# Local attention of six layers on one core: scores ahead of the last tile's weight turn, the next queries normalised ahead of the softmax's sums

## The reference

```python
q, k, v = split(shift_tokens(x) @ Wqkv[i])          # 16 heads of 64 channels
q = l2norm(q) * q_scale[i];  k = l2norm(k) * k_scale[i]
q = q * cos * scale + rotate_half(q) * sin * scale
k = k * cos / scale + rotate_half(k) * sin / scale
out = local_attention(q, k, v)   # windows of 32: each sees itself and the one before, softmax
x = out @ Wo[i] + x
x = feed_forward(shift_tokens(x)) + x               # layer norm, 341 hidden, gelu gate
```

## Time and profile before

| | |
|---|---|
| median of 3 runs | 3145.54 us (3144.41 to 3152.8) |
| the profiled execution | 3135.21 us, its span 3133.4 us |
| granted TensorE clock, mean | 0.971 |
| TensorE busy | 2802.7 us, 89% of the span |
| VectorE busy | 2594.8 us, 83% |
| ScalarE busy | 2238.7 us, 71% |
| GpSimd busy | 1365.0 us, 44% |

### The profile page before, as it was taken

The page is one execution under the profiler, slowest core; times in us unless marked ns, Lnnn a source line. Parts: engine busy times, 40 slices in busy tenths (PEclk is TensorE's granted clock), DMA queues, the critical chain, the costliest instruction groups (busy, mean ns, idle before and its releaser), DMA issues. The chain is left out here.

```text
span 3133.4 us, 74866 instructions
## 1 busy us (share of the span) xinstructions
PE 2802.7 (89%) x29085; PEld 1564.2 (50%) x29181; DVE 2594.8 (83%) x3866; ACT 2238.7 (71%) x3690; POOL 1365.0 (44%) x818
## 2 busy tenths in 40 slices
PE   3999898998898989879998998999899899999998
PEld 1233333333333333346655665666476656655764
DVE  4999889888887788469968996998699779968995
ACT  2277777767656667768867886887688778867884
POOL 0200333523335210056645664666466546646661
PEclk8699999999999999989999999999999999999999
DMA  3200001010010020011111111111111111111110
GB/s 112 69 1 2 1 8 32 1 32 8 9 32 2 21 68 2 2 39 41 36 43 43 35 35 44 42 35 57 29 35 36 57 29 35 35 50 35 39 38 21
DMA packets 62995, 101.21 MB, mean 32 GB/s; under 512 B 20450, under 2 KB 45216, under 8 KB 61472
## 3 DMA queue, kind: packets, MB, share of 16 engines
q1 hardware_dynamic: 62636, 96.26, 11.0%
HBM read 38.30 MB, written 7.34 MB: 15 GB/s over the span
## 5 line engine op out<-in xcount | busy, mean ns | idle before, releaser
L914 DVE TENSOR_REDUCE a_part<-ps 128x1 f32<-128x512 f32 (+3 forms) x1664 | 984.9, 652 | 157.8 <-PE ps L594 150.9
L890 ACT ACTIVATE a_Pb<-ps 128x1024 f32<-128x1024 f32 (+3 forms) x832 | 762.7, 974 | 347.8 <-PE ps L760 346.4
L1265 PE MATMUL ps<-early 128*128 128x512 f32 x1152 | 555.7, 615 | 76.7 <-DVE l_qn L1656 60.1
L1202 POOL TENSOR_TENSOR l_sine<-l_qn,stack 128x512 f32<-128x512 f32 x192 | 344.1, 1792 | 201.2 <-DVE l_qn L1656 193.5
L1226 POOL TENSOR_TENSOR l_weights<-l_weights,l_rcp 128x1024 f32<-128x1024 f32 x96 | 182.7, 1903 | 476.1 <-DVE l_rcp L1694 476.1
L594 PE MATMUL ps<-stack,a_QS 48*128 48x512 bf16 x1024 | 312.7, 405 | 72.2 <-DMA a_QS<-pieces 30.0
L1265 PEld LDWEIGHTS ps<-early 128*128 128x128 f32 x1152 | 205.0, 191 | 301.9 <-issue 144.9
L1645 DVE TENSOR_REDUCE l_norm<-l_square 128x8 f32<-128x512 f32 x384 | 252.8, 683 | 114.4 <-ACT l_square L1486 107.1
L1486 ACT ACTIVATE l_square<-ps 128x512 f32<-128x512 f32 x384 | 226.1, 594 | 89.0 <-PE ps L1265 87.8
L1665 DVE TENSOR_TENSOR l_cosine<-l_qn,stack 128x1024 f32<-128x1024 f32 x192 | 282.3, 1470 | 4.1
L644 PE MATMUL ps<-a_Pb,V 128*32 128x256 f32 (+1 forms) x3968 | 279.7, 398 | 0.0
(11 more groups left out here) (214 smaller groups left out, 5065.7 us busy)
## 6 DMA issues: line engine op xcount, KB each, us to landing
l_V_earlier<-l_V SPq DMA_DIRECT2D x96, 384.0 KB, 3.5
l_V_earlier<-l_V SPq DMA_DIRECT2D x96, 128.0 KB, 3.3
early<-in_L_ffn_Wqkv_dram SPq DMA_DIRECT2D x6, 1536.0 KB, 8.3
a_QS<-pieces SPq DMA_DIRECT2D x96, 64.0 KB
pieces<-a_piece SPq DMA_DIRECT2D x6, 512.0 KB, 2.6
pieces<-early SPq DMA_DIRECT2D x12, 256.0 KB, 2.7
a_KS<-pieces SPq DMA_DIRECT2D x48, 64.0 KB
l_w_o<-in_L_ffn_Wo_dram SPq DMA_DIRECT2D x6, 512.0 KB, 4.0
```

The source lines that it names most:

```text
L890: e.activation(Pb[:, n % 2, 2 * p:2 * p + 2, lo:CH], ps[:, 2 * p:2 * p + 2, lo:CH], ACT.Exp)\
L914: e.tensor_reduce(part[:, u % 2, column(h, qt), b:b + 1], bank[:, 0:width], AX.X, ALU.max)\
L1202: e.tensor_tensor(sine[:, :, 0:ROT], swap[:, :, ROT:LD], table[:, :, 0:ROT], ALU.mult).then_inc(s.rotated, 1)
L1265: e.matmul(ps[:, (V_BANK[T] if i == 2 else 0) + b, :], XS[:, T * P:(T + 1) * P], w_qkv[:, at:at + CH], start=True, stop=True).then_inc(s.v ...
```

## The change

The order of the instructions of `attend` is changed on three engines; no instruction is added, removed or altered.

- TensorE: `scores(T)` go ahead of `turn_weights(T - 1)`, and the projection of the queries of `T + 2` goes ahead of `values(T - 1)`.
- ScalarE: `place_low(T - 1, 0)` goes behind the inverse norms of the keys of `T + 1`; `store_o(T - 1)` goes behind the exponentials and the inverse norms of the queries of `T + 2`.
- VectorE: `place_high(T - 1)` goes behind `subtract(T)`; `normalise` of the queries of `T + 2` goes ahead of `sums(T)`.

```diff
--- before.py
+++ after.py
@@ -1376,17 +1376,17 @@
                         if ahead:
                             project(l, T + 1, 1, 0)
                             project(l, T + 1, 1, 1)
+                        scores(l, T, 0)
+                        scores(l, T, 1)
                         if T:
                             turn_weights(l, T - 1, 0)
                             turn_weights(l, T - 1, 1)
-                        scores(l, T, 0)
-                        scores(l, T, 1)
+                        if T + 2 < NT:
+                            project(l, T + 2, 0, 0)
+                            project(l, T + 2, 0, 1)
                         if T:
                             values(l, T - 1, 0)
                             values(l, T - 1, 1)
-                        if T + 2 < NT:
-                            project(l, T + 2, 0, 0)
-                            project(l, T + 2, 0, 1)
                         if ahead:
                             project(l, T + 1, 2, 0)
                             project(l, T + 1, 2, 1)
@@ -1559,21 +1559,20 @@
                         if ahead:
                             squares(l, T + 1, 1, 0)
                             squares(l, T + 1, 1, 1)
-                        if T:
-                            place_low(l, T - 1, 0)
                         if ahead:
                             inverse_norms(l, T + 1, 1)
                         if T:
+                            place_low(l, T - 1, 0)
                             place_low(l, T - 1, 1)
-                        if T:
-                            store_o(l, T - 1, 0)
-                            store_o(l, T - 1, 1)
                         if T + 2 < NT:
                             squares(l, T + 2, 0, 0)
                             squares(l, T + 2, 0, 1)
                         exponentials(l, T)
                         if T + 2 < NT:
                             inverse_norms(l, T + 2, 0)
+                        if T:
+                            store_o(l, T - 1, 0)
+                            store_o(l, T - 1, 1)
                         if ahead:
                             store_values(l, T + 1)
                     place_low(l, NT - 1, 0)
@@ -1723,20 +1722,21 @@
                             residual(l, T - 2)
                         if ahead:
                             sum_squares(l, T + 1, 1)
-                        if T:
-                            place_high(l, T - 1, 0)
                         if ahead:
                             normalise(l, T + 1, 1)
                         maxima(l, T)
                         subtract(l, T)
+                        if T:
+                            place_high(l, T - 1, 0)
                         if T + 2 < NT:
                             sum_squares(l, T + 2, 0)
                         if ahead:
                             cosines(l, T + 1, 1)
                             add_rotated(l, T + 1)
+                        if T + 2 < NT:
+                            normalise(l, T + 2, 0)
                         sums(l, T)
                         if T + 2 < NT:
-                            normalise(l, T + 2, 0)
                             cosines(l, T + 2, 0)
                     residual(l, NT - 2)
                     centre(l, 0)
```

## The result

The changed kernel is slower: 3197.4 us median of 4 runs (3186.35 to 3205.33) against 3144.97 us, a ratio of 1.0159 (95% interval 1.013 to 1.0188). The forecast was 3179 us in a range of 3150 to 3207. In the changed kernel VectorE's lines from `sum_squares` to `place_high`, and `residual`, stand one line higher (the cosines are L1664, the reciprocal L1693).

A forecast was written before the change was run, and what follows sets the result against it. A ring of waits over GpSimd's sequence was to set the pace: tiles from 15.32 to 15.64 us gave 25 us, layer starts 7, ends 1. Sum +33 on 3145.5: 3179 us, range 3150 to 3207.

The forecast's parts named there:

- GpSimd's sequence behind the reciprocal: Product, two sines, addition, two sines of the next keys; ends 10.63 us after the reciprocal, with 1.83 us of slack.
- the meeting at the port: VectorE's cosines and GpSimd's sines of the keys exclude each other at the SBUF port; sines end 0.95 us later.
- the hold: The wait of keys' cosines and sines for each other, 0.95 us; rival without it: 3105 us, chance 0.09.
- the ring: Steady tile, reciprocal to reciprocal over GpSimd's sines, add_rotated, normalisation and sums: 15.64 us instead of 15.32; chance 0.73.
- a ring of 15.8: Upper end of the forecast case in which GpSimd's ring sets the pace, priced at 3192 us.
- the 0.22: Wait of add_rotated after the end of GpSimd's second sine, some 0.22 us, read from a layer's last tile.
- The order at the port: Queries' cosines ahead of GpSimd's product, keys' cosines between the two sines; the order was said hardly to matter.
- A hold for the whole instruction: Rival: each hand-over at the port costs the full instruction, giving 16.06 us a tile and 3211 us; chance 0.07.
- TensorE's ring: Rival: TensorE's steady-tile ring, maxima through values, projections and scores, sets the pace at 15.20 us; 3144 us, chance 0.11.
- What scores ahead are worth: With scores ahead of the turn of weights on TensorE, maxima could start about 1.04 us sooner in each tile.
- The end of a layer: Reciprocal of tile 13 to the last turn of weights: 27.7 us instead of 27.54, 1 us for six layers.
- The start of a layer: The reciprocal of tile 0 comes 1.20 us later in each layer, 7 us for six layers.

The follow-up runs named there:

- e5: The changed kernel, but from a layer's tile 1 on VectorE sums the keys by heads into a spare tile instead of multiplying by the cosine table: 3179.02 us.
- e1: The changed kernel with VectorE's normalisation of the next queries put back behind the softmax's sums: 3181.38 us.
- e3: The changed kernel with sums ahead of the next queries' normalisation, and VectorE's copy of the turned weights ahead of the maxima in every tile: 3097.68 us.
- e4: The kernel before with one move alone, VectorE's normalisation of the next queries ahead of the softmax's sums: 3301.83 us.
- e2: The changed kernel with VectorE's copy of the turned weights ahead of the maxima in a layer's last two tiles alone: 3177.93 us.
- e6: The kernel before with only the next queries' projection ahead of values on TensorE and store_o late on ScalarE: 3113.52 us.

## Why the prediction was right, point by point

**The bound.** Right. GpSimd's sequence behind the reciprocal had 1.83 us of slack, the meeting at the port and the normalisation used 0.95 + 1.20 of it, and the tile came out at 15.64 us, as worked out. e5 takes the hold out, and the ring shows bare at the start of a layer, at 14.66 us where 14.69 was due. e1 takes the normalisation out, and the wait for GpSimd goes; the bare ring of 14.44 on the path forecast is not seen there. Single links were off by about 0.1 us in both directions: the held product ended 2.83 us after the reciprocal (forecast 2.94), the last sine 11.46 (11.58), and the normalisation starts 0.03 us after the addition's end instead of overlapping it. That such errors cancel to the second decimal is luck. So is, in part, that the time lies in the range: the tiles gave 22.0 of the 25 us forecast, and the starts and ends of the layers 33.8 where 8 was forecast. (3192, the price of a ring of 15.8, should be 3191.)

Two readings rested on rows that don't carry them. The cosines at 1884.43 took their full 1.23 us, so they hardly waited behind a sine, and the idling ahead of 1887.00, from which I took the 0.22, is put down to TensorE's turn (L1281). The changed kernel bears both out: its held cosines ran ahead of the next sine, and 0.22 us lie between the end of the last sine (2030.16) and `add_rotated` (2030.38).

**The order at the port.** Right: cosines ahead of the product, then first sine, cosines, second sine. The page "SBUF — State Buffer" of the Trainium skill, section "Who interferes with whom", says that issue order decides who blocks, and the trace agrees: the cosines, queued at 2027.32, went ahead of the sine of 2027.91. A hold for the whole instruction would have made 16.06 us by the prediction's estimate, and the 1.09 us that the held cosines took after the sine's end say why it was 15.64. The same section of the Trainium skill says that a VectorE instruction with at most one input from SBUF, outside its 2-port modes, does not contend with GpSimd; e5 agrees, with 1.28 us for the sine beside such a reduction.

**TensorE's ring.** Mis-sized by 0.19 us (15.39 for 15.20), and its closing wait misplaced. It hid behind GpSimd's ring in the changed kernel, as forecast, and capped e1 and e5. Its cause is the copy behind the subtraction: e3 moves it ahead and the ring is gone.

**What scores ahead are worth.** I priced the move as a gain of TensorE's that the other ring hides. e4 shows that the normalisation without the other moves costs far more, since the product then stands ahead of the scores, the values and the queries' projection; I had not followed that ring. Whether the scores' move or the projection's opens it is not shown, so what scores ahead are worth stays open.

**The end of a layer.** The term that failed: 1 us for six layers, 19.3 measured. I had priced the new order of instructions at their durations of before, and missed that in the steps of tiles 14 and 15 `values` have no projection of queries ahead of them to hide the wait for the copy (2.52 and 2.49 us of idling above). The clock I had priced at nothing; behind that idling it fell to its lower level, in all six ends. e2 takes the idling away and gets 19.5 us back in the median (3197.4 to 3177.9). The 1 us either way that I allowed was too narrow.

**The start of a layer.** The reciprocal of tile 0 came 2.4 us later on average, where 1.2 was forecast for the normalisation; e1, which takes it out, gives 1.35 a layer back. The rest goes along with the granted clock, which fell at the start of each of the six layers and of two in the kernel before, and with TensorE's first turn in the second to fifth layer, which starts after 2.5 to 3.1 us of idling at the loop's jump instead of 1.05 to 1.4. The kernels with a changed order on TensorE show this idling (e2, e3 and e5, and e1 and e6 in three of four layers), e4 with the old order doesn't, though its clock fell at all six starts too. No experiment tells what makes the jump longer, or what each of the two costs; this is open.

## What to carry to other kernels

Before a step is put ahead of another on one engine, follow what waits for the later one once around the ring: here 1.2 us of VectorE's own time stood ahead of a reciprocal from which two thirds of a tile of GpSimd's work hang, and the row that decides is the slack of that sequence, not the idle time of the busiest engine. Where two engines share a port, an instruction that moves also moves the meeting: price both orders of the meeting, and see whether it lies in the ring. And look at the first and last turns of a loop by themselves, since the work that covers a wait in the middle may not exist there.

## What the runs showed of the hardware that was not expected

TensorE's granted clock fell behind idling of a few microseconds inside a busy kernel. Behind idling of 2.52 us in the step of tile 14 it was at 0.64 on average from 1912 to 1916, while the steady tiles of the changed kernel, with idling of 0.6 to 1.4 us ahead of `values` in each, were granted 1.00. Where e2 took the idling away, the second layer's end was granted 1.00. Each stretch at the lower level in the layers lasted 3.4 or 6.8 us, and each of the six ends in the changed kernel's trace holds one or two of them.
